# A graph-transformer layer on one core: reordered project loop, shorter tile and token stages, node rows loaded beside the softmax, six of thirteen mixer products made there

## The reference

```
xn  = layernorm(x)
Q,K,V = (xn + 0.1*query_emb) @ (Wq, Wk, Wv) + b          # 4 heads of 64
scores = sum(Q[dst] * (K[src] + 0.2*rel_w[type])) / 8    # edges x heads
w   = segment_softmax(scores, dst);  agg = segment_sum(w * V[src], dst)
gnn = layernorm(where(deg > 0, agg, V) @ Wo + bo + xn) * gamma + beta
q,k,v = xn @ Wqkv.T; k, v normed per head of 64          # 8 heads
mix = (q @ (k.T @ v) / N) @ Wout.T + bout
x1  = x + gnn + mix
H   = gelu(layernorm(x1) @ W1 + b1)                      # 1024 wide
p   = softmax(H @ Wg + bg); e = argmax(p)                # 8 experts
out = x1 + p[e] * (H @ Wd[e] + bd[e])
```

## Time and profile before

| | |
|---|---|
| median of 3 runs | 2914.6 us (2912.91 to 2915.53) |
| the profiled execution | 2914.57 us, span 2912.7 us |
| busy share | PE 76%, DVE 62%, POOL 51%, PEld 49%, ACT 29% |
| mean granted TensorE clock | 0.842 of full speed |
| HBM traffic | 467.46 MB read, 175.42 MB written |

### The profile page before, as it was taken

One profiled execution on the slowest core, in us unless ns is written; L12 is line 12 of the kernel. 1 busy time (PEld: TensorE's weight loads), 2 busy tenths in 40 slices (PEclk: granted clock), 3 DMA queues, 4 the chain that ended last, 5 costly groups with the idle time before them and its releaser, 6 DMA issues. The chain is left out here.

```text
span 2912.7 us, 50277 instructions
## 1 busy us (share of the span) xinstructions
PE 2207.1 (76%) x11362; PEld 1413.3 (49%) x11363; DVE 1818.6 (62%) x3103; ACT 842.6 (29%) x2742; POOL 1497.4 (51%) x1474
## 2 busy tenths in 40 slices
PE   6872676576667676666676749999977999967997
PEld 3431333343333333333343337777765665546886
DVE  5662766676767666766676787888867667451111
ACT  2430110110111110110110147777753555522221
POOL 3555555565555555555555407777756434123442
PEclk9995777877787776787777869999998999989998
DMA  4545878788878878878778819888864444355451
GB/s 149 183 162 171 270 249 273 261 260 271 267 246 279 272 252 269 268 246 275 259 249 277 224 61 312 277 278 282 278 205 135 155 168 153 114 183 195 171 173 56
DMA packets 381054, 642.82 MB, mean 221 GB/s; under 512 B 39963, under 2 KB 228895, under 8 KB 380869
## 3 DMA queue, kind: packets, MB, share of 16 engines
q1 hardware_dynamic: 302900, 379.54, 39.3%
q0 software_dynamic: 77824, 262.55, 27.9%
q10 hardware_dynamic: 272, 0.00, 0.0%
HBM read 467.46 MB, written 175.42 MB: 221 GB/s over the span
## 5 line engine op out<-in xcount | busy, mean ns | idle before, releaser
L737 POOL DMA_INDIRECT s_kv<-kv_d,s_index x832 | 798.7, 960 | 634.5 <-issue 320.2
L868 PE MATMUL s_q_ps<-q,s_is_dst 128*128 x2496 | 514.4, 324 | 407.4 <-DVE s_key L791 293.6
L868 PEld LDWEIGHTS s_q_ps<-q,s_is_dst 128*128 128x128 bf16 x2496 | 211.1, 105 | 568.8 <-issue 501.8
L1288 PE MATMUL a_sum_ps<-a_w,a_is_dst 128*128 128x260 f32 x1760 | 403.6, 388 | 20.5 <-DVE sums L1259 11.9
L787 DVE TENSOR_TENSOR s_key<-s_kv,s_rel_ps 128x1024 f32<-128x1024 f32 x208 | 252.5, 1214 | 223.5 <-remote 211.2
L1201 POOL TENSOR_TENSOR a_w<-a_v,a_w 128x512 f32<-128x512 f32 x220 | 299.3, 1366 | 164.9 <-ACT a_w L1161 108.5
L1288 PEld LDWEIGHTS a_sum_ps<-a_w,a_is_dst 128*128 128x128 f32 x1760 | 328.0, 191 | 96.0 <-issue 25.1
L1177 ACT ACTIVATE a_w<-a_v,a_w 128x64 f32<-128x64 f32 x1100 | 285.9, 335 | 2.9 <-DMA a_v<-v_d 2.8
L686 ACT COPY scores<-s_part 128x32 f32 (+1 forms) x104 | 22.6, 218 | 831.9 <-issue 645.7
L873 PE MATMUL s_rel_ps<-rel,s_is_kind 64*128 64x64 bf16 x2496 | 241.7, 208 | 27.5 <-issue 27.5
L1235 DVE SCALAR_TENSOR_TENSOR a_is_dst<-node_of,first_node,a_col_ps 128x256 f32<-128x256 f32 x440 | 208.8, 475 | 82.8 <-PE a_sum_ps L1288 65.0
(11 more groups left out here) (310 smaller groups left out, 2970.7 us busy)
## 6 DMA issues: line engine op xcount, KB each, us to landing
a_v<-v_d SPq DMA_DIRECT2D x440, 256.0 KB, 3.8
v_d<-s_kv SPq DMA_DIRECT2D x208, 512.0 KB
s_local<-local_d SPq DMA_DIRECT2D x106, 256.0 KB
xh_d<-h_hid SPq DMA_DIRECT2D x24, 1024.0 KB, 7.0
s_kind<-type_d SPq DMA_DIRECT2D x212, 64.0 KB
s_kv<-kv_d,s_index POOLq DMA_INDIRECT x832
kv_d<-pkv SPq DMA_DIRECT2D x50, 256.0 KB, 2.0
wd<-in_L_ffn_Wd SPq DMA_DIRECT2D x8, 1024.0 KB, 11.9
```

The source lines that it names most:

```text
L737: nc.gpsimd.indirect_dma_start(out=kv[:, g * GROUP + b, :], out_offset=None, in_=R["kv"], in_offset=bass.IndirectOffsetOnAxis(ap=index[:, ...
L868: nc.tensor.matmul(q_ps[b][:, u, :], is_dst[:, h, e], M["q3"][:, bass.ds(regs[g % GROUPS * GROUP + u], 1), j, :] .rearrange("p a c -> p (a ...
L1288: ins = nc.tensor.matmul(sum_ps[(g * PAIRS + k) % BANKS][:], is_dst[:, g % WRING, 2 * k + u, :], w[:, g % WRING, 2 * k + u, :], start=(u = ...
```

## The change

1. **Project.** `normalise` is split: the statistics of block g+2 come before the value addition of g, the rest after it, and the wait for the last `xn` store moves down to the write of `xn`. SP's pair "load x, store xn" of a block (`rows_done`) moves to the end of the turn that makes the block.
2. **Tiles.** `dst` and `type` are cast, `src` is copied back and `local` is cast on ACT; validity is one product instead of two comparisons; PE turns `src` as soon as it is there; the stores wait for their own table only.
3. **Softmax.** SP also loads six quads of `xnt` (`MIXED`, quads 3 to 8), V of quads 0 and 1, `Wo` and four vectors of the node stage; PE makes the six mixer products in twelve halves between its other work, ACT copies them out, SP stores them in `mixed_d`.
4. **Aggregate.** POOL clears 40 semaphores of the node stage at its start.
5. **Nodes.** No `fresh` block. No V(0), V(1), `Wo` or vector loads; the rest of quad 1 is loaded right behind that of quad 0. Waits for the gate's weights move from the start to step 3. For quads 3 to 8 neither `xnt` is loaded nor a product made: `z` comes from `mixed_d`.
6. **Route.** 49 blocks instead of 52, the choice is made on the logits beside the `exp`, the two counting matmuls are bf16, fewer table steps; the weighting moves from POOL to ACT (49 ACTIVATEs of 128x56) and DVE (7 products of 128x392). The wait for the experts' weights moves into the experts stage.

```diff
 # stage_project, sync and vector
+            for u in range(2):
+                rows_done(u, u)
             with sp.Fori(0, TURNS) as i:
...
+                    rows_done(g + 2, u)
...
                 nc.vector.bn_aggr(mv[:], stats[:]).then_inc(S["mv_ready"], 1)
+                if value is not None:
+                    add_value(w, value)
 
                 dve.wait_ge(S["std_ready"], n + 1)
 # stage_softmax, sync
+            for j, q in enumerate(MIXED):
+                sp.dma_start(mix_x[:, j], R["xnt"][q * QUAD:(q + 1) * QUAD].rearrange("b p n -> p b n")).then_inc(xnt_in[j // 3], 16)
+            nodes = M["nodes"]
+            for q in range(2):
+                sp.dma_start(nodes["v"][:, q], quad(R["kv"][:, C:], q)).then_inc(nodes["v_in"][q], 16)
...
+            for j, q in enumerate(MIXED):
+                sp.wait_ge(S["mixed_copied"], 2 * (j + 1))
+                sp.dma_start(quad(R["mixed"], q - MIXED.start), mix_z[:, j % 4]).then_inc(mixed_out[j % 2], 16)
 # stage_softmax, tensor
+            def product(i):
+                j, m = divmod(i, 2)
+                pe.wait_ge(xnt_in[j // 3], 48)
+                if i >= 2:
+                    pe.wait_ge(S["mixed_copied"], i - 1)
+                for b in range(2):
+                    for k in range(KC):
+                        ins = nc.tensor.matmul(vw_ps[:, 2 * m + b, :], mix_x[:, j, 2 * m + b, k * P:(k + 1) * P],
+                                               M["z"][:, k, :], start=(k == 0), stop=(k == KC - 1))
+                ins.then_inc(S["mixed_done"], 1)
 # stage_nodes, sync and tensor
+                    if s in MIXED:
+                        sp.dma_start(z[:, s % 2], quad(R["mixed"], s - MIXED.start)).then_inc(z_in[s % 2], 16)
...
-                if 0 <= s - 1 < NQ:
+                if 0 <= s - 1 < NQ and s - 1 not in MIXED:
                     mixer(s - 1)
 # stage_route
+            for c, lo in enumerate(chunks):
+                act.wait_ge(S["tiles_hot"], c + 1)
+                act.wait_ge(S["chosen"], 1)
+                for b in range(lo, lo + CHUNK):
+                    ins = nc.scalar.activation(placed_value[:, b, 1, :], tile_hot[:, b, :], ACT.Copy,
+                                               scale=value[:, 1, b:b + 1])
```

More of the change, by code:

```diff
@@ L269, in normalise @@
                 dve.wait_ge(S["rstd_ready"], n + 1)
+                if value is not None:
+                    dve.wait_ge(xn_out[w], out)
                 nc.vector.tensor_scalar(xn[:, w, :], x[:, w, :], mv[:, 0:1], rstd[:], ALU.subtract,
@@ L553, in _ @@
-            for b in range(4):
+            nc.vector.tensor_scalar(src_f[:], field(0), 0.0, None, ALU.max).then_inc(S["src_set"], 1)
+            dve.wait_ge(S["dst_set"], 1)
+            nc.vector.tensor_tensor(local[:], dst_f[:], wide(blk_node), ALU.subtract).then_inc(S["local_set"], 1)
+            dve.wait_ge(S["local_set"], 1)
+            then(nc.vector.scalar_tensor_tensor(out=low[:], in0=local[:], scalar=-float(P - 1), in1=local[:], op0=ALU.add,
+                                                op1=ALU.mult))
@@ L554, in _ @@
+            then(nc.vector.tensor_scalar(valid[:], low[:], 0.0, -float(1 << 20), ALU.is_gt, ALU.mult))
+            nc.vector.tensor_tensor(by_tile(M["segment"]), dst_f[:], valid[:], ALU.add).then_inc(S["seg_set"], 1)
+            for b in (2, 3):
                 dve.wait_ge(S["turned"], b + 1)
-                to = (M["src"] if b < 2 else M["node_of"])[:, 0:TS_ROWS, :].rearrange("p r c -> p c r")
+                to = M["node_of"][:, 0:TS_ROWS, :].rearrange("p r c -> p c r")
                 c = 4 * (b % 2)
@@ L962, in _ @@
             ins.then_inc(S["ends_turned"], 1)
+            for i in range(5, 7):
+                product(i)
             pe.wait_ge(S["ends_ready"], 2)
@@ L966, in _ @@
             ins.then_inc(S["carry_turned"], 1)
+            for i in range(7, 10):
+                product(i)
             pe.wait_ge(S["copied"], n_bank)
@@ L1360, in stage_nodes @@
             uses += [("tokens", step - 4, c) for c in range(6, HC)] if here(4) else []
-            uses += [("mixer", step - 1, m) for m in range(len(halves(step - 1)))] if here(1) else []
+            uses += [("mixer", step - 1, m) for m in range(len(halves(step - 1)))] if here(1) and step - 1 not in MIXED else []
             uses += [("tokens", step - 3, c) for c in range(HALF_C)] if here(3) else []
@@ L1601, in second_moments @@
                 dve.wait_ge(S["y_scaled"], q * 2 + 2)
-                dve.wait_ge(S["swap_copied"], after("mixer", q))
+                if q in MIXED:
+                    dve.wait_ge(z_in[w], 16 * len([p for p in MIXED if p <= q and p % 2 == w]))
+                else:
+                    dve.wait_ge(S["swap_copied"], after("mixer", q))
                 if q >= 2:
```

361 lines of the change are left out of this document (204 added, 157 removed).

## The result

The changed kernel takes 2845.16 us (median of 4 runs, 2843.84 to 2845.41), the kernel before 2915.07 (4 runs, 2912.91 to 2916.81): ratio 0.976, 95% interval 0.9743 to 0.9777. The profiled execution took 2843.84 us, with a span of 2841.9 us. The forecast was 2842 us.

The account below looks back on a forecast made before the run. Bounds were taken stage by stage: scores half the time and unchanged, PE in steady node steps, DVE in softmax and route. Terms -25 - 4.4 + 0.5 - 12 - 20.7 - 11 = -72.6 from 2914.57 gave 2842 us, range 2830 to 2860.

Parts of the forecast that it names:

- Project: Project stage: statistics ahead of the value addition take some 1.3 us off the chain, PE becomes the limit; -25 us.
- if POOL becomes project's limit: Project stage: a stated sign that the prediction is wrong; DVE and POOL were expected to fit in 3.10 us a turn.
- All waits gone are 28: Project stage: ending PE's waits for `pxn`, 50 x 0.56 us, gives 28 us, the upper bound of the gain.
- Tiles: Tiles stage: gathered rows to last copy falls from 12.7 to 8.3 us; -4.4, between -3 and -5.
- Softmax: Softmax stage: added mixer product halves nearly fit between PE's other work; +0.5 us, from -1 to above +7.
- rival B: Softmax stage: five product halves run at 1.2 GHz and hold the small turn; +7 us, 2849; chance 0.06.
- Ramp: Node stage's start: earlier loads and a shorter barrier bring PE's turn of step 3 forward; -12, between -6 and -16.
- Steady steps: Node stage: six steps lose their mixer product, 3.45 us each; -20.7, between -14 and -23.
- Route: Route stage: 6.2 us less up to the first one-hot, shorter chunks without POOL; -11, between -7 and -13.
- Scores and aggregate: Both stages: no change expected; a move above 3 us in either would show the prediction wrong.
- Rival A: Project stage: `pxn`, held by POOL or load waits, keeps PE short of its limit; 13 us less gain, 2855; chance 0.13.
- Rivals C to F: C, another node-stage loop limits, 2856, 0.10; D, more gain, 2828, 0.07; E, scores slower, 2940, 0.01; F, no effect, 0.01.

Follow-up runs that it names:

- the two edits: Changed kernel with two buffers for GpSimd's query remainder, its end-of-block wait dropped, and without SyncE's surplus load and store in project: 2839.28 us, ratio 0.9698.
- the run with the hold: Changed kernel with three places for loaded x, xn, xnt, and GpSimd waiting for VectorE's second norm of quad 0: 2463.14 us, ratio 0.9690.
- unrelated buffers: Changed kernel with two more GpSimd operations in each route chunk, on buffers nobody else reads: 2483.01 us, ratio 0.9764.
- the run with three places: Changed kernel with three places instead of two for loaded x, xn, xnt in the node stage, so quad 2 loads earlier: 2475.74 us, ratio 0.9738.

## Why the prediction was right, and where not

- **Project, -25 forecast, -23.0 measured.** The number was near, the mechanism wrong, and by its own sign ("if POOL becomes project's limit") this term failed. "Some 1.3 us leave the chain, more than the 0.74 that PE idled, so PE becomes the limit": the limit that took over was GpSimd's chain, of which I had counted the busy time (2.14 us) and not the four handovers (0.9 us more). And TensorE's own turn is 2.93 us or less, not 3.10, because busy time with modelled ends holds waits. The rows had a sign of that: 165 us of the loop with 46 turns are 3.59 a turn, and 3.59 less the 0.56 of waiting is 3.03; the 3.83 that I wrote for a turn has the loop's first and last microseconds in it. "All waits gone are 28" was thus too little for TensorE (the two edits bring -36.5) and too much for this kernel. The end cost 3.0 us and not 2, by GpSimd's late turn; SyncE's surplus pair, that I had named, was covered. I had given the move on SyncE no term of its own, when the whole gain hangs on it (+54 us without). That -23.0 came so near -25 is luck: a limit that I had not seen stood near the one that I had set too high.
- **Tiles, -4.4, measured -3.9.** Right within the bounds.
- **Softmax, +0.5, measured -0.3.** The products are hidden, and the small turns came at the old places. The granted clock was 1.00 under the first halves, so rival B did not come.
- **Ramp, -12, measured -13.3.** Right: 2.6 of it is the barrier (0.92 instead of 3.55 us from the start of the last sum to the first load; forecast 2.4), the rest the loads.
- **Steady steps, -20.7, measured -23.4.** Mis-sized, and just past its bound of -23: some 3.8 us a step and not 3.45. "PE's one wait in a step is 0.40 us" came from a single row, the shortest of seven; the others had up to 1.26. The wait came of GpSimd's addition beside VectorE's scaling. That cause rests on ten steps of two kernels, in which wait and slow scaling go together to 0.01 us, and on the run with the hold, where a step with its product and without the meeting took 29.73. There GpSimd's addition fell at another time because of the third places; no run moves that addition alone.
- **Route, -11, measured -11.0.** 12.94 us to the first one-hot (forecast 12.9), chunks of 2.08 (forecast 2.2). That GpSimd's work was what made VectorE slow is now shown with unrelated buffers. The rule cited there, of the Trainium skill, "SBUF — State Buffer", section "SBUF: two separate sides", agrees: VectorE's one-hots took 1.90 and 1.26 us beside GpSimd and 1.08 and 0.56 alone.
- **Scores and aggregate, 0, measured +2.6 and +0.7.** Under the 3 us that I had set as the mark of being wrong, and within what one code varies; whether scores took something back is open.
- **Rival A** (project stops short of TensorE's limit, 0.13) is in part what happened, by another mechanism: not by `pxn` (0.41 to 0.46 us from 62 us on) but by GpSimd's query. I had named that only as a sign of error. The rule of the Trainium skill, "SBUF — State Buffer", section "SBUF: two separate sides", that an operation of VectorE in a two-port mode can be kept out for a whole one of GpSimd's, I had set aside by the earlier trace rows ("411 to 419 ns whatever POOL did"). That reading was wrong. No row tells the mode, but the times agree with the rule. In those turns `pxn` started 0.40 us or more behind an operation of GpSimd of 0.67, which ended 0.05 to 0.27 us later, early enough to cost nothing. Where the two start together, it does cost. The changed kernel has such a turn:

```profile
57.48 0.67 POOL L337 TENSOR_TENSOR q<-pqr,q 128x256 f32 x1 [0.22 <-POOL q L334]
...
57.50 0.80 DVE L285 TENSOR_SCALAR pxn<-px,pmv,prstd 128x256 f32<-128x256 f32 x1
```

  `pxn` ends 0.15 us behind GpSimd's end. The kernel before had one of 0.68 us at 40.26, outside the window of the earlier trace rows, and its node stage showed the full size, on the same norm that was slow in the run with three places (1.38 us when GpSimd idles):

```profile
2241.11 8.93 DVE L1615 TENSOR_SCALAR n_x<-n_x,n_mv,n_rstd 128x256 f32<-128x256 f32 x4
```

- **Rivals C to F** did not come. Three misses (+2 in project, +2.6 in scores, -4 in the node stage) nearly cancel, so that the whole came within 2 us is luck too.

## What to carry to other kernels

Ask of a chain that may become the limit how long one round of it takes with its handovers, not how busy it is: four short operations that wait for each other made GpSimd the limit when it was two thirds busy (108.8 of 168.4 us). When statistics or other reads move ahead in a loop, their load must move as well. A steady duration in one loop does not show that two engines do not disturb each other: look where their operations start together. And where GpSimd and VectorE both work in SBUF, giving GpSimd its work earlier can cost more on VectorE than the wait that it ends. Here the earlier load lost 3.6 us in the node stage, and with a wait that keeps GpSimd off four short operations of VectorE it won 4.9.

## What the runs showed of the hardware that was not expected

The same scores code took 1453 to 1472 us in the first six profiles and 1081 to 1086 in the eight after them, on other chips; the other stages differ by at most 2.4 us where their code is the same. No chip was seen at both speeds, so that it is the chip, and not something else that went with it, is inferred. Busy time of 250 us of it in the changed kernel and, from the run with three places, on the faster chip (columns as in the earlier trace rows):

```profile
473.00:723.00 250.00, 172.31 (x1028) 90.72 (x1025) 169.88 (x199) 25.60 (x90) 139.36 (x147) 0.75 0.80 260
```

```profile
473.00:723.00 250.00, 213.68 (x1396) 117.57 (x1396) 231.82 (x274) 36.91 (x126) 189.61 (x199) 0.84 1.02 357
```

The stage's costliest operation on VectorE takes the same time there (1.21 us on both); TensorE's matmuls are a little shorter (303 ns in the mean and not 322, `s_q_ps`), at a granted clock of 0.84 and not 0.75. The gathers and stores move 357 GB/s and not 260. In each of the six slower profiles GpSimd once stood 7.9 to 8.3 us ahead of a gather with no releaser named (7.97 in the changed kernel); in the faster ones never over 0.32. What it waits for there no run shows. So a stage that lives on gathered rows has to be compared on one chip, and half of this kernel's time rests on it.
